# Row maxima of the cross-attention scores: from four banks of scores reduced by VectorE to a difference, a relu and one fused instruction, with the users of the shared PSUM bank placed anew

## What is computed

```
x = x + attn(layernorm(x))                      # one head
x = x + xattn(layernorm(x), ctx)                # 16 heads of 64, 1601 keys
x = x + block_on_31_positions(layernorm(x))     # a top-k choice of positions, attention, MLP
# in xattn, per batch and head:
sim = q @ k.T / 8 ; attn = softmax(sim) ; out = attn @ v ; out @ Wo + bo
```

## Time and profile before

| | us |
|---|---|
| median of 3 runs | 2567.93 |
| the profiled execution's own time | 2568.49 |
| its span, first to last instruction | 2567.2 |
| PE busy | 2224.8 (87%) |
| DVE busy | 2091.6 (81%) |
| POOL busy | 1742.3 (68%) |
| ACT busy | 1690.2 (66%) |
| mean granted TensorE clock | 0.949 of full |

### The profile page before, as it was taken

The page is one execution under the profiler, slowest core; times in us unless marked ns, Lnnn a source line. Parts: engine busy times, 40 slices in busy tenths (PEclk is TensorE's granted clock), DMA queues, the critical chain, the costliest instruction groups (busy, mean ns, idle before and its releaser), DMA issues. The chain is left out here.

```text
span 2567.2 us, 55548 instructions
## 1 busy us (share of the span) xinstructions
PE 2224.8 (87%) x22232; PEld 1627.5 (63%) x22232; DVE 2091.6 (81%) x3079; ACT 1690.2 (66%) x2835; POOL 1742.3 (68%) x980
## 2 busy tenths in 40 slices
PE   5898898988888889898988889888898988989984
PEld 3566665666666666665666666666665666667663
DVE  4888888888888878888888888888888888888973
ACT  2577676766766666676766667767676666767671
POOL 1477776776777666776777666766776766767782
PEclk8899999999999999998999999999999999999996
DMA  4000000000000000000000000000000000000000
GB/s 119 11 2 11 1 2 11 1 11 2 11 2 1 11 2 17 4 1 11 2 11 2 1 11 6 13 4 11 1 1 11 2 11 1 8 1 4 1 2 9
DMA packets 16959, 22.05 MB, mean 9 GB/s; under 512 B 5232, under 2 KB 14592, under 8 KB 16704
## 3 DMA queue, kind: packets, MB, share of 16 engines
q1 hardware_dynamic: 16704, 18.50, 2.3%
HBM read 16.27 MB, written 2.10 MB: 7 GB/s over the span
## 5 line engine op out<-in xcount | busy, mean ns | idle before, releaser
L1284 POOL TENSOR_TENSOR EL<-PF,EH 124x1024 f16<-124x1024 f32 x624 | 1497.4, 2414 | 304.4 <-ACT PF L736 220.8
L736 ACT ACTIVATE PF<-PS 124x512 f32<-124x512 f32 x1664 | 979.8, 596 | 505.6 <-PE PS L452 429.3
L906 DVE TENSOR_REDUCE pmax<-PS 128x1 f32<-128x806 f32 x1024 | 998.5, 989 | 254.2 <-PE PS L483 239.6
L466 PE MATMUL PS<-Ch,EH 123*128 123x97 f16 (+1 forms) x6656 | 798.9, 210 | 101.7 <-POOL EL L1284 70.7
L466 PEld LDWEIGHTS PS<-Ch,EH 123*128 123x128 f16 (+1 forms) x6656 | 621.8, 99 | 316.3 <-issue 142.5
L468 PE MATMUL PS<-Cl,EL 123*128 123x97 f16 (+1 forms) x6656 | 795.2, 210 | 0.0
L468 PEld LDWEIGHTS PS<-Cl,EL 123*128 123x128 f16 (+1 forms) x6656 | 611.9, 100 | 181.6 <-issue 17.4
L451 PE MATMUL PS<-AH,ChT 97*124 97x512 f16 x1664 | 660.8, 397 | 11.6 <-ACT PF L736 6.9
L452 PE MATMUL PS<-AL,ClT 96*124 96x512 f16 x1664 | 650.4, 391 | 0.0
L483 PE MATMUL PS<-ChT,AH 96*128 96x403 f16 x2048 | 547.4, 350 | 56.2 <-DVE AL L914 47.2
L892 DVE TENSOR_SCALAR EH<-PF 124x1024 f16<-124x1024 f32 x416 | 442.3, 1063 | 10.7 <-ACT PF L736 10.7
(11 more groups left out here) (209 smaller groups left out, 1576.9 us busy)
## 6 DMA issues: line engine op xcount, KB each, us to landing
Cf<-in_ctx SPq DMA_DIRECT2D x16, 599.6 KB
X<-in_x SPq DMA_DIRECT2D x16, 128.0 KB, 4.1
out_x<-X SPq DMA_DIRECT2D x16, 128.0 KB, 1.7
msk<-in_attention_mask SPq DMA_DIRECT2D x4, 256.0 KB, 4.5
AH<-mh SPq DMA_DIRECT2D x64, 2.0 KB
xWqT<-in_xWqT SPq DMA_DIRECT2D x2, 256.0 KB, 5.1
xWo<-in_xWo SPq DMA_DIRECT2D x2, 256.0 KB, 4.7
fw<-in_fw SPq DMA_DIRECT2D x2, 256.0 KB, 3.8
```

The lines of the kernel that those rows point to most:

```text
L466: pe.matmul(PS[:, 6, u0:u0 + DC + 1], EH[0:kr, r, qs], Ch[j][0:kr, t, :], start=(t == 0 and q == 0), stop=False, skip_group_check=True)
L736: act.activation(PF[:, n % PRING, :], PS[0:KP, 4 + n % 2, :], ACT.Exp).then_inc(sg("ex"), 1)
L906: dve.tensor_reduce(pmax[:, b % 2, ht, half:half + 1], PS[:, 2 * half:2 * half + 2, 0:NKEY], AX_XY, ALU.max).then_inc(sg("max_rd"), 1)
L1284: pool.tensor_tensor(EL[:, r - 1:r + 1, :], PF[:, f - 1:f + 1, :], EH[:, r - 1:r + 1, :], ALU.subtract).then_inc(sg("lo_pool"), 1)
```

## The change

The maximum over all keys of max(s1, s2), where s1 is a score against a key of the first half and s2 the score against its partner in the second half, is the maximum of s1 + relu(s2 - s1). s2 - s1 is a matmul against the difference of the two keys. So a `keys` step makes KD, the difference of the key halves (96 x 806, float16, by DVE, once per batch); `diff` multiplies the queries by KD into banks 2 and 3, and ACT applies relu into `over` in SBUF (two buffers); `base` multiplies by the first half into banks 0 and 1; `fold` is one tensor_tensor_reduce of DVE over 806 columns that adds `over` and bank 0/1 and gives the maximum. There are 512 of each. `redmax` is gone. ACT's copy of the placed maxima carries the sign.

DVE takes the rounding of three pairs in four, ACT of one in four. PF has 10 places instead of 8. AH and AL have one buffer instead of two. The steps on bank 7 get other places: `sel_rank` is cut into two counting steps and the rest, layernorm 0 runs a batch earlier, and the chosen block has six places a batch instead of eight.

```diff
-PRING = 8
+PRING = 10
-SA_PLACES = (5, 7, 16, 20, 29, 33, 46)
-TURN_PLACES = (31, 42, 55, 57)
-CHOSEN_PLACES = (59, 68, 72, 81, 83, 85, 94, 98)
-Q_LEAD, MAX_LEAD, ROW_LEAD = 38, 36, 8
+SA_PLACES = (4, 6, 8, 10, 30, 32, 56)
+SEL_PLACE = 34
+TURN_PLACES = (58, 60, 62, 64)
+SIGMA_PLACE = 71
+CHOSEN_PLACES = (82, 84, 86, 88, 90, 97)
+Q_LEAD, MAX_LEAD, ROW_LEAD = 38, 35, 9
...
# ahead(n)
-        c = chunks(n, h, h + EARLY)
...
-        todo += [(first - ROW_LEAD - 2, ("redmax", n, h, h + EARLY)), (first - ROW_LEAD, ("placemax", n, h, h + EARLY))]
+        start = 1 if n == 0 and h == EARLY else first - MAX_LEAD
+        for k, ht in spread(range(T * h, T * h + T * EARLY), start, first - ROW_LEAD - 3):
+            todo += [(k, ("diff", n, ht)), (k + 1, ("base", n, ht)), (k + 2, ("fold", n, ht))]
+        todo += [(first - ROW_LEAD, ("placemax", n, h, h + EARLY))]
# plan(b)
-                 (AV_LAG + 2 * KT + 2, ("sel_row", b - 1)), (AV_LAG + 2 * KT + 3, ("sel_rank", b - 1))]
+        todo += [(after, ("ln_stats2", b - 1)), (after + 2, ("sel_w", b - 1)), (SEL_PLACE, ("sel_row", b - 1)),
+                 (SEL_PLACE + 1, ("sel_count", b - 1, 0)), (SEL_PLACE + 3, ("sel_count", b - 1, 1)),
+                 (SEL_PLACE + 10, ("sel_rank", b - 1))]
...
+        todo += [(95, ("ln_stats0", b + 2)), (99, ("ln0", b + 2))]
...
+        todo += list(zip(TURN_PLACES, transposes_of(n))) + [(TURN_PLACES[1] + 3, ("keys", n))]
-        todo += list(zip((0, 3, *q[:6], q[5] + 2, q[5] + 5, q[6]), self_attention(n)))
+        todo += list(zip((*q[:6], q[5] + 4, q[5] + 10, q[6]), self_attention(n)[2:]))
# whole_order(): load_ctx at AV_LAG + 12 instead of AV_LAG + 8
# rounded(p)
-            return sg("eh_act" if p % 2 == 0 else "eh_dve"), p // 2 + 1
+            return (sg("eh_act"), p // 4 + 1) if p % 4 == 0 else (sg("eh_dve"), p // 4 * 3 + p % 4)
# TensorE
-                elif k == "max":
-                    b, ht, half = s.a
-                    w.wait_ge(sg("ct"), 4 * b + 2)
-                    w.wait_ge(sg("q_lo"), at["q", b, ht // 4])
-                    if i > 2:
-                        w.wait_ge(sg("max_rd"), i - 2)
+                elif k in ("diff", "base"):
+                    b, ht = s.a
+                    j, bank = b % 2, 2 if k == "diff" else 0
+                    w.wait_ge(sg("keys"), b + 1)
+                    w.wait_ge(sg("q_hi"), at["q", b, ht // 4])
+                    if i > 1:
+                        w.wait_ge(sg("relu" if k == "diff" else "fold"), i - 1)
...
+                    src = KD[j][:, :] if k == "diff" else ChT[j][0:DC, :, :].rearrange("p t k -> p (t k)")
                     for n in range(2):
+                        m = pe.matmul(PS[:, bank + n, 0:NKEY], AH[0:DC, ht * P:(ht + 1) * P],
+                                      src[:, n * NKEY:(n + 1) * NKEY], start=True, stop=True)
# ScalarE
+                elif k == "diff":
+                    w.wait_ge(sg("diff_mm"), i)
+                    if i > 2:
+                        w.wait_ge(sg("fold"), i - 2)
+                    act.activation(over[:, i % 2, :, :], PS[:, 2:4, 0:NKEY], ACT.Relu).then_inc(sg("relu"), 1)
# q on ScalarE and VectorE, and the DMA of placemax: one buffer of AH and AL
-                    if b >= 2:
-                        w.wait_ge(sg("st"), (b - 1) * TILES)
+                    if b >= 1:
+                        w.wait_ge(sg("st"), (b - 1) * TILES + (hp + 1) * KT)
# VectorE
+                elif k == "keys":
...
+                    dve.tensor_tensor(KD[b % 2][:, :], keys[:, 2 * NKEY:4 * NKEY], keys[:, 0:2 * NKEY],
+                                      ALU.subtract).then_inc(sg("keys"), 1)
+                elif k == "fold":
+                    w.wait_ge(sg("relu"), i)
+                    w.wait_ge(sg("base_mm"), i)
+                    o = over[:, i % 2, :, :]
+                    dve.tensor_tensor_reduce(out=o, in0=o, in1=PS[:, 0:2, 0:NKEY], scale=1.0, scalar=LEAST, op0=ALU.add,
+                                             op1=ALU.max, accum_out=pmax[:, b % 2, ht:ht + 1]).then_inc(sg("fold"), 1)
```

More of the change, by code:

```diff
@@ L60 @@
 SHIFT_ROW = 4096.0
+LEAST = -3.0e38
 PI = 3.1415925
@@ L167, in whole_order @@
             out.append(gm.pop(0))
+    out += [("keys", 0)] + self_attention(1)[:2]
     out += [step for _, step in sorted(ahead(0), key=lambda x: x[0]) if _ < 0]
@@ L194, in whole_order @@
     out += [("norm", B * HP - 1), ("turn_u", B - 1, QD - 1, 0), ("turn_u", B - 1, QD - 1, 1), ("proj", B - 1, QD - 1)]
-    out += [(k, B - 1) for k in ("ln_stats2", "sel_w", "sel_row", "sel_rank")]
+    out += [("ln_stats2", B - 1), ("sel_w", B - 1), ("sel_row", B - 1)]
+    out += [("sel_count", B - 1, 0), ("sel_count", B - 1, 1), ("sel_rank", B - 1)]
     out += [step for _, step in chosen(NG - 1)]
@@ L328, in build @@
         ClT = [sb(f"ClT{i}", [DC, KT, KP], F16) for i in range(2)]
-        AH = [sb(f"AH{i}", [DC + 1, H * S], F16) for i in range(2)]
-        AL = [sb(f"AL{i}", [DC, H * S], F16) for i in range(2)]
+        AH = sb("AH", [DC + 1, H * S], F16)
+        AL = sb("AL", [DC, H * S], F16)
+        KD = [sb(f"KD{i}", [DC, 2 * NKEY], F16) for i in range(2)]
+        over = sb("over", [P, 2, 2, NKEY])
         cmx = sb("cmx", [KP, 1])
@@ L404, in bank_of, with left @@
             return 7 if k < 0 else k % 8
+        def left(s):
+            return sg(SPARE[s.kind]), s.i * (T if s.kind == "sel_row" else 1)
         def freed(s):
@@ L411, in freed @@
                 return None
[L412 to L418, removed]
+            return left(spare[before])
+        fold_of = {s.a: s.i for s in order if s.kind == "fold"}
         def tensor_program():
@@ L426, in bank_free @@
                 if tail_from <= k < tail_from + 8:
-                    w.wait_ge(sg(SPARE[spare[tail_from - 1].kind]), spare[tail_from - 1].i)
+                    w.wait_ge(*left(spare[tail_from - 1]))
                     w.wait_ge(sg("u"), B * HP)
-                    w.wait_ge(sg("max_rd"), chunk_total)
+                    w.wait_ge(sg("relu"), len(fold_of))
+                    w.wait_ge(sg("fold"), len(fold_of))
                     w.wait_ge(sg("ex"), TOTAL)
@@ L736, in scalar_program @@
                     act.activation(PF[:, n % PRING, :], PS[0:KP, 4 + n % 2, :], ACT.Exp).then_inc(sg("ex"), 1)
-                elif k == "round" and s.a[0] % 2 == 0:
+                elif k == "round" and s.a[0] % 4 == 0:
                     n = 2 * s.a[0] + 1
@@ L885, in vector_program @@
                 k, i = s.kind, s.i
-                if k == "round" and s.a[0] % 2:
+                if k == "round" and s.a[0] % 4:
                     n = 2 * s.a[0] + 1
@@ L1090, in vector_program @@
                                       ALU.add).then_inc(sg("sel_w"), 1)
+                elif k == "sel_count":
+                    b, t = s.a
+                    j = b % 2
+                    row = PS[:, 7, 0:S]
+                    w.wait_ge(sg("sel_row"), b + 1)
+                    w.wait_ge(sg("const"), CONST_ALL)
+                    wt = X3[:, b % 4, t, D:D + 1]
+                    for c, op in enumerate((ALU.is_gt, ALU.is_ge)):
+                        dve.tensor_scalar(junk[:, 2 * t + c, :], row, wt, None, op, ALU.add,
+                                          accum_out=cnt[:, j, c, t:t + 1])
+                    dve.scalar_tensor_tensor(out=junk[:, 4 + t, :], in0=row, scalar=wt,
+                                             in1=lower[:, t, :, :].rearrange("p u q -> p (u q)"), op0=ALU.is_equal,
+                                             op1=ALU.mult, accum_out=cnt[:, j, 2, t:t + 1]).then_inc(sg("sel_cnt"), 1)
                 elif k == "sel_rank":
```

84 lines of the change are left out of this document (27 added, 57 removed).

## The result

| | before | changed |
|---|---|---|
| median, us | 2568.01 (7 runs) | 2552.78 (7 runs, 2545.62 to 2564.48) |
| ratio | | 0.9941 (95% interval 0.992 to 0.9961) |
| span of the profiled execution | 2567.2 | 2553.5 |
| PE idle in the span | 342.4 | 341.1 |
| mean granted clock | 0.949 | 0.960 |

The account below looks back on a forecast made before the run. PE was taken as nearest to full, busy 2224.8 of 2567.2 us, its gaps being waits; from 2568.5 us, -119.5 - 35 + 26 + 15 + 3 - 8 = -118.5 gave 2450 us, range 2385 to 2535.

Parts of the forecast that it names:

- fixed waits: PE's once-a-batch waits for AL, the counting, `sa_s`, `sa_f` and layernorm 0 go: -119.5 us, bounds -60 and -135.
- `lo` waits: PE's waits for the late float16 split on POOL and DVE, 83.9 us, shrink: -35 us, bounds +24 and -84.
- new waits: `base` behind the fold: PE's `diff` waits for the relu before and `base` for the fold before: +26 us, bounds 0 and +70.
- new waits: exp, U and UT: On ACT the next exp and the copy of U stand behind relu, delaying PE: +15 us, bounds 0 and +176.
- PE's busy time (clock): Fewer waits leave PE less time at the 1.2 GHz clock: -8 us, bounds 0 and -39.
- DVE, work: DVE's busy time falls by 231 us to about 1860, worth nothing by itself but making its steps less late.
- A rule against this: DVE's moved rounds and POOL's `lo` lock each other out: 59 us more on POOL, +24 on PE inside the `lo` term.
- the sign that this term is wrong: PE's waits for relu, fold, exp and U together exceeding 100 us would show the new-wait term wrong.
- moves waits only: Rival: each PE wait that goes uncovers POOL at its eight steps; 2573 us, no change; chance 0.05.
- The slower rival: PE pays for relu in ACT's queue, at 40% of its 439 us +176, giving 2611 us; chance 0.09.
- half felt: Rival: PE pays 15% of relu's 439 us on ACT; 2501 us, about 2510 with fixed waits at -100; chance 0.18.
- nearly all waits go: Rival: nearly all PE waits vanish, -218 us to 2350, taken with half that surplus as 2385; chance 0.14.

Follow-up runs that it names:

- x2: The changed kernel's new places, ten places of PF and single AH, with the old maxima and rounding shared half and half: 2464.46 us, 0.9598 of the kernel before.
- x12: x2 with the maxima waiting for AL again, as in the kernel before: 2468.10 us, 0.9602 of the kernel before.
- x1: Changed kernel with ACT rounding every second pair again, half and half with DVE: 2500.12 us, 0.973 of the kernel before.
- x5: x2 with three quarters of the rounding on DVE: 2538.29 us, 0.9896 of the kernel before.
- y3: x10 with three quarters of the rounding on DVE: 2486.76 us, 0.9686 of the kernel before.
- y1: Changed kernel, but the one pair in four that ACT rounds is one whose `lo` is POOL's, not DVE's: 2520.73 us, 0.9819 of the kernel before.
- x8: Changed kernel with the fold one step earlier in the list, right behind `base`: 2505.04 us, 0.9764 of the kernel before.
- x7: x2 with eight places of PF instead of ten: 2463.53 us, 0.9611 of the kernel before.
- x10: Changed kernel with rounding half and half, fold one step earlier, and the copy of U ahead of the round: 2422.56 us, 0.9421 of the kernel before.
- x11: x2 with the copy of U ahead of the round in the list: 2437.85 us, 0.9482 of the kernel before.
- x4: Changed kernel with the old places of the other users of bank 7: 2571.44 us, 1.0016 of the kernel before.
- x6: x2 with DVE's rounding in the form that also writes an accumulator: 2512.59 us, 0.9794 of the kernel before.
- y4: Changed kernel with rounding half and half and the fold one step earlier, but the old places: 2573.49 us, 1.0022 of the kernel before.

## Why the prediction was wrong

In the prediction's own terms, from the profiles of both kernels (us):

| term | forecast | measured |
|---|---|---|
| fixed waits | -119.5 | -121 |
| `lo` waits | -35 | +7 |
| new waits: `base` behind the fold | +26 | +70 |
| new waits: exp, U and UT | +15 | +60 |
| all other waits and idle time of PE | +3 | -18 |
| PE's busy time (clock) | -8 | -12 |
| sum | -118.5 | -14 |

The steps that failed are the new waits, by 89 us, and the `lo` waits, by 42.

- **Fixed waits (-119.5): right in kind.** All five are gone from the trace, and x2 shows that the places are worth 103 us. Of its reasons one was wrong: the 45 us for AL did not hang on the dependence (x12).
- **DVE, work (-231, measured -73.8): wrong too.** It was no term of the sum, but the relief that the `lo` term leaned on. Fold was put at 1.08 and is 1.063. The failure is "208 more rounds at 1.063". DVE's rounding grew by 736.5 - 442.3 = 294 us instead of 221, its `lo` by 60, `keys` took 28, and two small instructions grew by 26 (L888) and 30 (L1129). The split of the context (L963 in the old kernel) became cheaper, by 41. The reductions that went were 998.5 us in the earlier trace rows, not the 1013 of count times mean. I took a mean that contained waiting as if it were a price per piece.
- **A rule against this (59 us on POOL, +24 on PE): right rule, wrong quantity.** I priced the lock by its length, and POOL's busy time indeed rose by only 16 us. The cost lies in lateness: DVE's rounds last up to 2.67 us and what stands behind them in its queue waits, and where the same round is what POOL's next `lo` needs, the two take turns. POOL's 42.3 us behind L892 in the earlier trace rows became 275.4. x1, x5 and y3 put the moved rounding at 2.1 to 3.0 points, y1 somewhat over half of the 2.1 to which pair is moved. The split between the lock, the order and DVE's amount of work stays open.
- **New waits (+26 and +15, measured +70 and +60): failed most.** `base` behind fold is 78.9 where the old reductions had 8.7, and the exp, U and UT are 23.2 + 44.8 + 13.7 = 82 where they had 22. With the relu's 0.9 the fold, the exp and U make 148, above the 100 that I had named as the sign that this term is wrong. My argument was that two steps, 2.9 us, exceed a fold of 1.08. It looked at the fold alone and not at what stands ahead of it on DVE, a round of up to 2.67 us. x8 shows the size: one step of list order, 45 us. For the second part I named the relu as the cause, and that is wrong: without any relu x2 has 97 us of such waits.
- **`lo` waits (-35, measured +7): failed.** 91 us against 84. Of the reasons by which I had them fall, PF's two places carry nothing where they were tried (x7), and DVE's relief was a third of what I had. The places do help: in x2 they are 62. The inference that I tied to this sign, that POOL's own queue and not DVE makes them, is not borne out: with the moved rounding back on ACT they fall to 69 (x1).
- **U.** Its wait went from 14.5 to 72.9 us in x2, where PE waits less for others; I had no term for it beyond 15. About 30 us of it is the place of ACT's rounding in the list (x10, x11).
- **Rivals.** The nearest was "moves waits only" (2573, chance 0.05). It is also wrong as a rule: x2 shows that closing the gaps pays. Taken in this order, the result is a gain of 103 us by the places and then a loss of 88 by the rest; in the other order, the rest loses 4 us (x4) and the places gain 19. I had not held the two apart. The slower rival, PE paying for relu, is refuted, and so is the mechanism of "half felt", although PE's +60 us are 14% of relu's 439, near the 15% of that rival: ACT's load could rise to 2025 us with gain (x1), and the same waits are there without relu (x2). Relu brought no table loads: the 1.283 us loads are 10 in both traces, and the Trainium skill's "Table sets: the hidden batching unit" in "ScalarE: Activation LUTs" had it so.
- **Sums.** "Half felt" with fixed waits at -100 is about 2520, not 2510, and half of the surplus of "nearly all waits go" is 2400, not 2385. Neither changes the outcome.

What stays open: why 66 us more of steady DVE work cost 50 us in x6, by which path the choice of the pair in y1 reached PE, and how the remaining 70 of the places' 103 us are split among the other moves.

## What to carry to other kernels

A mean in which an engine waited inside its instruction is not a price: look at minimum, median and maximum, and at whose instruction has the length of the difference. Before work is moved to an engine, write down who waits for the moved piece and whom it waits for; a lock and a dependence between the same two engines can make them take turns. When a change has a part that lays out and a part that computes, price and run them apart, since here a good layout hid a costly sharing; and the order in which an in-order queue meets its work (fold one step earlier, U ahead of a round) was worth 45 and 30 to 39 us.

## What the runs showed that I had not expected

A VectorE instruction on 32 columns took 1.174 us in the mean (0.227 at the least, 2.117 at the most) beside a busy GpSimd, and 0.238 in the kernel before; whether it meets a `lo` of POOL is a matter of place (in y1, where POOL is as busy, its mean is 0.270). The form with an accumulator gave a spread of 0.04 us where the plain form had 2.01, and made the kernel 1.7 points faster at a longer median. And a kernel with 393 us less VectorE work (y4) ran no faster at all, with PE busy for longer at a lower granted clock.
